# Values by one product, residual by TensorE, Sinkhorn's transpositions moved into its products

## What is computed

```python
# Sinkhorn, 32 matrices of 128 x 128, up to 31 steps
v_new = c_ / jnp.maximum(jnp.einsum('bnm,bnk->bmk', K, u), EPS)
u_new = r_ / jnp.maximum(jnp.einsum('bnm,bmk->bnk', K, v_new), EPS)
# (after it: a routed feed-forward layer and a GRU over 32 steps)
# attention, 16 heads of width 8, in each of 128 batches of 32 tokens
qkv = (x @ w_qkv).reshape(b, n, 3, H, DK)
attn = softmax(einsum('bhnd,bhmd->bhnm', q, k) / sqrt(DK))
y = einsum('bhnm,bhmd->bhnd', attn, v)          # then y @ w_proj, added to x
# layer norm, and a mixture of experts that takes the best of 8 per token
logits = xf @ gate_w + gate_b
one_hot = one_hot(argmax(logits), E)
h = gelu(einsum('td,edh->teh', xf, w1)); y = einsum('teh,ehd->ted', h, w2)
```

## Time and profile before

| | us |
|---|---|
| median of 3 runs | 609.08 |
| lowest and highest | 604.85, 610.93 |
| the profiled execution | 608.91 |
| its span, first to last instruction | 607.2 |
| TensorE busy in it | 509.5 (84%) |
| VectorE busy | 361.9 (60%) |
| ScalarE busy | 283.4 (47%) |
| GpSimd busy | 152.4 (25%) |

### The profile page before, as it was taken

One profiled execution on the slowest core, in us unless ns is written; L12 is line 12 of the kernel. 1 busy time (PEld: TensorE's weight loads), 2 busy tenths in 40 slices (PEclk: granted clock), 3 DMA queues, 4 the chain that ended last, 5 costly groups with the idle time before them and its releaser, 6 DMA issues. The chain is left out here.

```text
span 607.2 us, 35608 instructions
## 1 busy us (share of the span) xinstructions
PE 509.5 (84%) x15374; PEld 417.6 (69%) x15374; DVE 361.9 (60%) x1219; ACT 283.4 (47%) x691; POOL 152.4 (25%) x270
## 2 busy tenths in 40 slices
PE   0899999999996998999999888789877871599995
PEld 0788888888884744666666677567666650599994
DVE  4655555555555765666665448369777777255552
ACT  5222212222212692555554545668666641477772
POOL 2111111111110000000000057334555556055553
PEclk9899999999997999999999987899899885599998
DMA  9060000000000036663230020000110012233430
GB/s 276 8 225 0 0 0 0 0 0 0 0 0 2 0 68 149 222 194 71 71 87 1 1 75 1 4 4 0 37 37 31 29 64 102 75 91 94 119 106 22
DMA packets 22656, 34.39 MB, mean 57 GB/s; under 512 B 3617, under 2 KB 15910, under 8 KB 22217
## 3 DMA queue, kind: packets, MB, share of 16 engines
q1 hardware_dynamic: 19824, 27.23, 16.2%
q0 software_dynamic: 2784, 6.56, 3.1%
HBM read 25.98 MB, written 8.26 MB: 56 GB/s over the span
## 5 line engine op out<-in xcount | busy, mean ns | idle before, releaser
L230 PE MATMUL ps_u<-v_cur,buf_b 128*32 128x32 f32 x7936 | 78.4, 198 | 1.9 <-DVE v_cur L292 1.3
L230 PEld LDWEIGHTS ps_u<-v_cur,buf_b 128*32 128x32 f32 x7936 | 74.7, 110 | 5.3 <-DVE v_cur L292 1.4
L215 PE MATMUL ps_v<-buf_a,u_pad 128*32 128x128 f32 x1984 | 62.9, 281 | 7.2 <-issue 5.9
L215 PEld LDWEIGHTS ps_v<-buf_a,u_pad 128*32 128x32 f32 x1984 | 54.3, 113 | 10.9 <-issue 9.2
L586 PE MATMUL ps_h<-buf_c,up 128*128 128x512 f32 x96 | 50.9, 627 | 0.5 <-DVE buf_c L802 0.3
L1731 POOL DMA_INDIRECT out<-yb,token_i x39 | 38.6, 991 | 48.8 <-DVE resid L1833 47.7
L195 ACT ACTIVATE over<-u_diff 128x32 f32<-128x32 f32 x31 | 7.1, 230 | 89.6 <-POOL u_diff L175 89.6
L179 POOL TENSOR_TENSOR u_hist<-inv_u,r_sum 128x16 f32 x62 | 13.7, 221 | 137.7 <-DVE inv_u L299 137.7
L1294 POOL TENSOR_TENSOR vb<-vn,row_mask 128x1024 f32<-128x1024 f32 x16 | 30.2, 1890 | 52.8 <-DVE var L1582 27.1
L1754 PE MATMUL m_h<-xT,w_near 128*128 128x128 f32 x312 | 43.1, 283 | 0.0
L1764 PE MATMUL m_y<-w,hid_t 128*128 x312 | 42.2, 279 | 0.1
(11 more groups left out here) (310 smaller groups left out, 1135.5 us busy)
## 6 DMA issues: line engine op xcount, KB each, us to landing
cw_b<-cw_d SPq DMA_DIRECT2D x16, 512.0 KB, 8.0
xt<-sorted_x SPq DMA_DIRECT2D x39, 136.0 KB
w<-in_w SPq DMA_DIRECT2D x2, 2048.0 KB, 17.0
buf_a<-in_x SPq DMA_DIRECT2D x4, 512.0 KB, 6.1
buf_b<-in_x_t SPq DMA_DIRECT2D x4, 512.0 KB, 7.0
buf_d<-in_x_nt SPq DMA_DIRECT2D x1, 2048.0 KB, 9.0
sorted_x<-nobody SPq DMA_DIRECT2D x1, 1088.0 KB, 4.6
out<-yb,token_i POOLq DMA_INDIRECT x39
```

Of the source, the lines that this page charges most:

```text
L215: last = mm(ps_v[h][32 * j:32 * j + 32, 0:D], u_pad[:, h, j, 32 * i4:32 * i4 + 32], K[:, g * D:(g + 1) * D], start=i4 == 0, stop=i4 == TI - 1)
L230: last = mm(rows_u[h][32 * q:32 * q + 32, g, :], KT[:, b * N:(b + 1) * N], v_cur[:, h, k:k + 1].broadcast_to([P, WIDE]), start=True, stop= ...
```

## The change

1. Values: `values` makes one product of 128 x 256, the values with the channel on the partitions, in place of 32 products of 32 x 32. VectorE turns its 32 x 32 blocks from PSUM into vn (`turn_values`), which gives the same vn as before; ScalarE's `values_out` goes.
2. Residual: `project_output` adds the tile's rows with a product with the identity into the same PSUM, and ScalarE copies the result into rows (`rows_out`, where `values_out` stood); VectorE's `add` goes.
3. GpSimd: `place_values` no longer waits for `scales` or `moments`. It still waits for the values in vn and for the mixing two chunks back.
4. VectorE's routing steps: `moments` moves to even chunks ahead of the transposition, `scales` has three steps instead of four and moves to odd chunks ahead of `choose`, its last step (`shifts`) goes behind `choose`; two casts are written by the reduction itself. ScalarE's `inverse_root` moves to odd chunks.
5. Sinkhorn: on TensorE the transposition of half 0 stands in the middle of half 1's column products and that of half 1 behind the first part of half 0's row products. On VectorE `invert` of half 0 stands ahead of `clamp` of half 1; in the first turn both inversions stand ahead of the last two `scale_by_c`.

```diff
-                    for h in range(HALVES):
-                        pe.wait_ge(u_ready[h], i + 1)
-                        to_columns(h)
-                    for h in range(HALVES):
-                        pe.wait_ge(v_den[h], i + 1)
-                        turn(h)
-                    for h in range(HALVES):
-                        pe.wait_ge(v_ready[h], i * 2 + 1)
-                        pe.wait_ge(s["kt_scaled"], 2 * h + 2)
-                        to_rows(h, 0)
-                        pe.wait_ge(v_ready[h], i * 2 + 2)
-                        to_rows(h, 1)
+                    pe.wait_ge(u_ready[0], i + 1)
+                    to_columns(0, range(TI))
+                    pe.wait_ge(u_ready[1], i + 1)
+                    to_columns(1, range(TI // 2))
+                    pe.wait_ge(v_den[0], i + 1)
+                    turn(0)
+                    to_columns(1, range(TI // 2, TI))
+                    pe.wait_ge(v_ready[0], i * 2 + 1)
+                    pe.wait_ge(s["kt_scaled"], 2)
+                    to_rows(0, 0)
+                    pe.wait_ge(v_den[1], i + 1)
+                    turn(1)
+                    pe.wait_ge(v_ready[0], i * 2 + 2)
+                    to_rows(0, 1)
...
@@ VectorE, first turn @@
                 clamp(0, 0)
+                invert(0, 0)
                 clamp(1, 0)
-                invert(0, 0)
+                invert(1, 0)
                 scale_by_c(2)
                 scale_by_c(3)
-                invert(1, 0)
...
@@ GpSimd @@
                     if c + 1 < NC:
-                        if c >= 4 and c % 2 == 0:
-                            pool.wait_ge(row_ends, c // 2 - 1)
-                        if c >= 3 and c % 2 == 1:
-                            pool.wait_ge(summed, c // 2)
                         place_values(c + 1)
...
@@ TensorE, values and project_output @@
-                    for b in range(CB):
-                        for r in range(R):
-                            last = mm(ps_v[32 * r:32 * r + 32, b * N:(b + 1) * N], xs[:, k, b, :],
-                                      w_qkv[:, 2, 32 * r:32 * r + 32], start=True, stop=True)
-                    last.then_inc(v_mm, 1)
+                    mm(ps_v[:, 0:CT], w_qkv[:, 2, :], xs[:, k], start=True, stop=True).then_inc(v_mm, 1)
...
-                        last = mm(ps_p[:, g * WIDE:(g + 1) * WIDE], o_t[:, k, g * P:(g + 1) * P], w_proj[:], start=True, stop=True)
+                        mm(ps_p[:, g * WIDE:(g + 1) * WIDE], o_t[:, k, g * P:(g + 1) * P], w_proj[:], start=True, stop=False)
+                        here = rows[:, c * 2 + g, 0:WIDE] if isinstance(c, int) else rows[:, bass.ds(c * 2 + g, 1), 0:WIDE]
+                        last = mm(ps_p[:, g * WIDE:(g + 1) * WIDE], ident[:], here, start=False, stop=True)
...
@@ ScalarE @@
-                def values_out(c):
-                    act.wait_ge(v_mm, c + 1)
-                    if c >= 2:
-                        act.wait_ge(v_out, c - 1)
-                    nc.scalar.copy(vn[:, c % 2, :], ps_v[:, 0:CT]).then_inc(v_read, 1)
+                def rows_out(c):
+                    act.wait_ge(p_mm, c + 1)
+                    nc.scalar.copy(rows[:, 2 * c:2 * c + 2, 0:WIDE], ps_p.rearrange("p (t d) -> p t d", d=WIDE)).then_inc(x2_done, 1)
...
@@ VectorE @@
-                def add(k):
-                    dve.wait_ge(p_mm, k + 1)
-                    here = rows[:, 2 * k:2 * k + 2, 0:WIDE]
-                    tt(here, ps_p.rearrange("p (t d) -> p t d", d=WIDE), here, ALU.add).then_inc(x2_done, 1)
+                def turn_values(k):
+                    dve.wait_ge(v_mm, k + 1)
+                    if k >= 2:
+                        dve.wait_ge(v_out, k - 1)
+                    v.transpose(vn[:, k % 2, :], ps_v[:, 0:CT]).then_inc(v_read, 1)
...
                     if i >= 4 and i % 2 == 0:
+                        moments(i // 2 - 2)
+                    if i >= 5 and i % 2 == 1:
                         scales(i // 2 - 2)
-                    if i >= 5 and i % 2 == 1:
                         choose(i // 2 - 2)
-                    if i >= 2:
-                        add(i - 2)
+                        shifts(i // 2 - 2)
+                    turn_values(i + 1)
                     if i >= 1:
                         over_sum(i - 1)
                     if i >= 2:
                         spread(i - 2)
-                    if i >= 3 and i % 2 == 1:
-                        moments(i // 2 - 1)
```

More of the change, by code:

```diff
@@ L1610, in place @@
                     c.step(tt(eq[:, gs, :], ranked[:, 0:PAIR, :], hot[:], ALU.mult))
-                    c.step(v.tensor_reduce(slot[:, gs], eq[:, gs, :], AX.X, ALU.add))
-                    v.tensor_copy(tables.slot_i[:, gs], slot[:, gs]).then_inc(slots_done, 1)
+                    with nc.allow_low_precision(reason="one nonzero term of each sum"):
+                        v.tensor_reduce(tables.slot_i[:, gs], eq[:, gs, :], AX.X, ALU.add).then_inc(slots_done, 1)
                 dve.wait_ge(made, MASKS + 1)
+                turn_values(0)
                 for i in range(NC - 1):
@@ L1676, in _ @@
                 c.step(tt(places[:], places[:], expert[:].rearrange("p (w k) -> p w k", k=PACK), ALU.mult))
-                c.step(v.tensor_reduce(count[:, 0:TABLE // PACK], places[:], AX.X, ALU.add))
-                c.step(v.tensor_copy(tables.packed_i[:], count[:, 0:TABLE // PACK]))
+                with nc.allow_low_precision(reason="whole numbers below two to the power of 24"):
+                    c.step(v.tensor_reduce(tables.packed_i[:], places[:], AX.X, ALU.add))
 def experts(nc, io, consts, late, tables, w1, w2, w_ready, sorted_x):
```

39 lines of the change are left out of this document (24 added, 15 removed).

## The result

The changed kernel took **586.7 us** (median of 6 runs, 581.5 to 590.3); the kernel before took 610.6 (median of six runs, three of them those of the table above). The ratio is **0.959**, 95% interval 0.954 to 0.965, so 24 us or 4.1% faster; the ratio leaves out the changed kernel's longest run, 1.5% above its fastest. Its profiled execution took 586.56 us (span 584.8), 22.4 less than the profiled 608.91. The forecast was 593 (586 to 604), a gain of 16: side and place right, the size too small. The median stands just inside the range, but the ratio does not: 0.959 of the 609.08 that the forecast started from is 584.4.

The account below looks back on a forecast made before the run. TensorE (busy 509.5 of 607.2 us) was taken as the main bound, with TensorE and VectorE about equal in the changed chunks; 12.5 - 1.5 + 2.0 + 3 = 16.0 us off 609.08 gave 593, range 586 to 604.

Parts of the forecast that it names:

- The stall: Attention chunks with stores: TensorE's small value products break beside GpSimd's stores; 11.1 us of stall, 1.4 a chunk, would go.
- The first rival: Attention chunks with stores: the stall moves into the mixing, 604 us if all of it, 599 if half; chance 0.17.
- Chunks 7 to 15: 8 x (7.86 - 6.3) = 12.5: Attention chunks with stores: each falls from 7.86 to 6.3 us, 12.5 us won over eight.
- Chunks 0 to 7: 1.5 lost: Attention chunks without stores: chunks 2 to 6 each lose 0.3 us, 1.5 us lost.
- Transposition: 0.424 taken: VectorE's 128x256 transposition of the values from PSUM: 0.424 us each, bounds 0.385 and 0.85.
- The rival at 0.85: Attention: the transposition costs 0.85 us and VectorE becomes the sole bound, 599 us; chance 0.08.
- Sinkhorn: 3 won: Sinkhorn: 30 turns fall from 5.32 to 5.17 us, 4.5 won; less the first turn's loss, 3 us won.
- End of the attention: 2.0 won: From the last maximum to the last slots: VectorE drops 2.4 us of steps, GpSimd is nearly the bound; 2.0 us won.
- The slower case: Attention: GpSimd's product meets VectorE's small chains, 1.9 us lost in each of 13 chunks, 618 us; chance 0.05.

Follow-up runs that it names:

- a_stream_2: The changed kernel with the old 32 small value products and ScalarE's copy of them, on a long-gap chip: 599.0 us (one run), kernel before 606.9.
- b_values_2: The kernel before with only the values changed (one product, turned by VectorE), on a long-gap chip: 595.3 us (one run), kernel before 606.9.
- b_stores_end: The kernel before with all indirect stores moved behind the last two mixings, none inside the chunks: 612.3 us (one run), kernel before 592.3.
- b_same: The kernel before, unchanged, traced on another chip: 592.1 us (one run), median there 593.1.
- a_same: The changed kernel, unchanged, on other chips: 582.3 us, ratio 0.985 to the kernel before; repeated as a_same_2, 582.9 us (one run).
- b_sink: The kernel before with the Sinkhorn part of the change alone: 586.0 us, ratio 0.989 to the kernel before.
- a_both: The changed kernel with a_copy's move and VectorE's old order in the first Sinkhorn turn: 580.9 us, ratio 0.983; repeated as a_both_2, 579.7 us.
- a_copy: The changed kernel with the copy of the next input moved from GpSimd to ScalarE: 582.1 us, ratio 0.982 to the kernel before.
- a_late: The changed kernel with its indirect stores held back to lie beside the mixing: 585.1 us, ratio 0.985 to the kernel before.

## Where the prediction failed, and what it had right

**The stall.** Right for the comparison that it was made for. The 11.1 us of waits went whole, and the runs bear out the cause that it named: a stream of small products beside GpSimd's indirect stores. On chip D the gaps stand in whichever stream lies beside the stores (the values in a_stream_2, whose mixing takes its 0.66 us, the mixing in b_values_2) and they end with the stores: the first trace and those of chip D have 31 streams beside stores with such gaps before the last maximum, and in 30 of them the last gap ends 0.28 to 0.50 us behind the last store's instruction (in the 31st the stream ends first). Without stores the short gaps of chip A are gone (b_stores_end). What it could not know from one trace is that the size of the term changes from chip to chip. The kernel before took 609 and 607 us in two series and 591 to 593 in four. Between the first trace and b_same 14.6 of 16.9 us lie in chunks 7 to 15. The changed kernel hardly notices: 586.7 in the first series, 582 to 583 on two chips; of the 5.8 us between the spans only 0.3 lie in chunks 7 to 15, and 2.1 in chunks 0 to 7, where its first trace has the lower clock for longer. So of 24 us 8 to 11 are won where the gaps are short, and the rest only where they are long.

**The first rival** (the stall moves into the mixing, 0.17) did not come about, for the reason that the prediction gave: the stores are over when the mixing begins. That 41 to 55 pieces pass first is no protection by itself, as b_values_2 shows. It was closer than 0.17 makes it look: 448.52 against 448.52, while gaps come up to 0.5 us behind a store, and each of these mixings takes 0.1 to 0.2 us more than an undisturbed one. So the place in time was partly luck. In the first trace the changed kernel has such a gap only behind the last maximum, 0.59 us at 472.90, in the mixing that starts at 471.63 beside a store.

**Chunks 7 to 15: 8 x (7.86 - 6.3) = 12.5.** This is the step that failed: 6.3 us a chunk was too long. Measured: 5.95, so 15.3. The 6.3 were VectorE's 6.05, against TensorE's 5.9, and 0.25 for mutual waits of the two. VectorE's own figure was near (5.56 busy a chunk and not 5.7, 5.95 with all that lies between its instructions). TensorE's was not: its chunk was to grow by 0.28 and did not (next paragraph). And the wait was charged on top of a mean, though the chunks are of two kinds: one of 6.5 us, where VectorE never waits and TensorE stands 0.75 before the rank, as the prediction had it in kind (0.6), and one of 5.4, where TensorE is the bound. Their mean has no room for the 0.25. Of the 7.86 some 0.25 a chunk was the lower clock (2 us in eight, the estimate above), so some 2 us of both the forecast and the measured gain of this term are not the change's.

**Chunks 0 to 7: 1.5 lost.** Measured 0.1 won in the first pair of traces, 2.2 on chip B. The forecast gave TensorE 0.28 more a chunk. Between the starts of its products (before, a chunk without stores: values to projection 0.76, projection to mixing 0.66; after 0.43 and 1.02) the residual costs 0.36 and not 0.53, and the values give 0.33 and a further 0.09 ahead of them, and not 0.25. The sum is near zero, and both kernels run their short undisturbed chunks in 5.30 us. The 39.44 of the first trace has a granted clock of 0.91: its first two chunks took 5.55 and 5.80 in place of the 4.14 and 4.97 of a_same. The gap of 1.3 us inside the scores, which both traces of the kernel before have and those of the changed kernel lack, was in no term.

**Transposition: 0.424 taken, 0.447 measured** (bounds 0.385 to 0.85). The rival at 0.85 is out.

**Sinkhorn: 3 won.** Measured 5.2, by b_sink 6.2. The row products start where the forecast had them (2.27, measured 2.29), but 2.27 + 2.38 + 0.16 + 0.31 is 5.12 and not the 5.17 written: a slip of 0.05, times 30 turns 1.5 us. And the first turn lost 0.8 (0.2 between b_same and a_same), not 1.5; a_both takes 0.4 less for it than a_same, a_both_2 0.8 less than a_same_2. The mechanism was only half right: the stalls were to fall from 0.57 to 0.42 and measure 0.24 + 0.31 = 0.55. What got shorter is the issue. From the first column load to the end of the first transposition has 38.62 - 36.72 = 1.90 us, the changed kernel 33.97 - 31.99 less the stall of 0.24, so 1.74. That the end of the turn still came out is luck.

**End of the attention: 2.0 won.** Measured 2.3 (19.5 to 17.2), 2.0 on chip B.

**Sum.** 16.0 and 2.8 (chunks 7 to 15), 1.6 (chunks 0 to 7), 2.2 (Sinkhorn), 0.3 (end), less 0.5 in between: 22.4. All three larger misses go the same way: a cost for TensorE that was too high, a wait added for safety, a slip, and one gap that no term had.

**The slower case** (GpSimd's product beside VectorE's small chains) did not come: the product starts behind the transposition, which stands behind the chains. The steps that did stretch are those beside the copy, 0.41 to 0.44 us for 0.19, as the earlier trace rows had it for another; with the copy gone (a_copy) they are back at 0.19. The Trainium skill, page "SBUF — State Buffer", section "SBUF: two separate sides", tells of such a lock between VectorE and GpSimd; this case's 411 to 435 ns beside the copy and 191 without it agree with it.

**Left open.** Why the same program has gaps of 0.56 us in two series and of 0.1 to 0.2 in four, and whether that is the chip's. The profile puts both down to TensorE's issue; DMA packets of the stores take the same time in the traces of both kinds (0.13 us). Nothing here shows what in a store stops TensorE. Whether the changed kernel would pay for stores beside the mixing where the gaps are long is not known: a_late met only short ones. The parts that free GpSimd's product and move the routing steps (3 and 4) were never run alone, so what they give or cost is not known.

## What to carry to other kernels

A stall that one trace shows steadily, chunk after chunk, may still belong to the machine: take the kernel's time on a few chips before a large term is put on it. Keep long streams of small products clear of GpSimd's indirect stores by place in time as well as by form, since the gap goes to whichever stream lies there. Where chunks are of two kinds, work out each kind's bound by itself and take the mean last: an engine that never waits in the list of waits can still be the bound of only half of them. Test the parts of a change one by one and also the whole without each part: here the residual paid only together with the values.

## What the runs showed of the hardware beyond that

- The first and last of the 64 weight loads of the 32 value products start 0.54 us apart where nothing disturbs them (b_same). Beside an indirect store the stream is broken for 0.1 to 0.2 us, or not visibly, in four series, and in two (609 and 607 us) for 0.56 to 0.61 us, every 0.73 us until soon after the last store.
- The products with large operands (128x136, 128x256) beside the same stores had no such gap in the first trace of the changed kernel.
- A VectorE step with two inputs of 128x32 elements took 411 to 435 ns where it met GpSimd's 0.41 us copy (a_same), and 191 without it; GpSimd's stores alone did not stretch it (a_copy).
